# Flamingo layer with routed zones: a ring of eight places for the zone weights, four fixed loads a body, and the last body's weights scaled while they are rounded

## The chip, the cores and the metric

The kernel runs on one core of a Trainium2 chip. What counts is the device time of one execution in microseconds (us), as the median of several runs. Engines are named as in the profile: PE is TensorE (PEld its weight loads), DVE VectorE, ACT ScalarE, POOL GpSimd, SP SyncE, which here only issues DMAs; "SPq" rows are those issues.

## What is computed

For 8 images: a layer norm, cross attention of 112 queries to 375 context rows (16 heads of 16), a gated residual; then a layer norm, a router that picks 3 of 8 zones per image, and for each of them a hidden layer of 1024 with Gelu, weighted and added.

```python
x = x + tanh(g_xattn[0]) * xattn(layernorm(x), ctx, ctx, mask, Wq, bq, Wk, bk, Wv, bv, Wo, bo)
# _L0_ffn_ref(x): called with layernorm(x)
pooled = x.mean(axis=1)
h = jnp.tanh(pooled @ W1 + b1)
logits = h @ W2 + b2
probs = jax.nn.softmax(logits, axis=-1)
top_p, top_i = jax.lax.top_k(probs, TOP_K)
top_w = top_p / top_p.sum(axis=-1, keepdims=True)
for e in range(N_ZONES):
    z = jax.nn.gelu(x @ Wa[e]) @ Wb[e]
    zone_outputs = zone_outputs + z * w[:, e, None, None]
x = x + tanh(g_ffn[0]) * (x + zone_outputs)
```

x is 8 x 112 x 256, Wa is 8 x 256 x 1024 and Wb 8 x 1024 x 256, all in float32. The products need more than float16's precision, so keys, queries, the hidden layer and the zone weights are held as two float16 numbers, a high part (the value rounded) and a low part (what the rounding left).

## The kernel before, in words

**Two phases.** In the first, attention runs image by image while all zone weights are fetched, scaled by 64 (WSCALE) and split into high and low halves in SBUF (`wa`, `wb`). In the second, 24 pairs of image and zone run one after the other: `g1` (L1370) and `g2` (L1397) are 48 matmuls each of 128x128 by 128x112.

**Bodies and slots.** The first phase is a loop over b from -1 to 7, written out by hand for every engine; each engine has its own instruction stream and waits on semaphores. A body has four slots. In slot s of body b TensorE makes the transposed scores of image b for one group of heads (`st_tile`, L1159 and L1163, three tiles), the plain scores of image b+1 (`s1`, L1147), from which VectorE takes row maxima (L866), the product with the values (`pv`, L1181), and some small work of images b+2, b and b-1 between (context transposes L1190, key and query projections L1199 and L1225, value projection L1208 and others). ScalarE does the exponentials (L597).

**Keys and queries through DRAM.** The keys of image b+2 are projected in slots 0 and 1 of body b. ScalarE rounds them (L697), VectorE makes the low part (`k_lo`, L908), SP writes both to DRAM (`write_k`, L341, one call for each half) and reads them back in another layout (`read_k`, L352, and `read_q`, L305). The first `s1` of body b+1 needs the reads of heads 0 to 7 of image b+2. The row maxima take a like way: ScalarE copies them to `ms`, SP copies them into `rq` (`move_max`, L361), and `st_tile` of the next body reads `rq` in L1159.

**Zone weights.** The weights are 64 parts of 128 x 512 float32, eight per zone: four of Wa, four of Wb. A load (`load_parts`, L373 for Wa, L376 for Wb) brings two parts, 512 KB, into two places of the ring `stage`, which has six. For each part GpSimd scales it in place (`scale_part`, L503, one slot ahead), ScalarE rounds it into `wa` or `wb` (`w_hi`, L707), and GpSimd subtracts the rounded from the scaled (`lo_part`, L508), which frees the place. Each slot of bodies 0 to 7 finishes two parts; parts 56 to 63 (LATE and on) belong to body 7, and their low parts are made by VectorE (`lo_late`, L961). SP calls `load_parts` four times a body, two slots ahead of ScalarE; each call waits until the two places are free. SP works its stream strictly in order, so what stands behind a waiting call waits as well.

**The seam.** After body 7 everything waits for the last weights. VectorE reads the number of the first zone from `idx_row` into a register (L996, in `copy_weights`), copies that zone's Wa from `wa` to `wqkvo` and `qbd` (L998 and L999), and TensorE starts `g1(0)`. `hidden` on ScalarE does the Gelu (L800) and the weighting (L802).

## Time and profile before

| what | value |
|---|---|
| median of 3 runs | 319.05 us (318.33 to 320.27) |
| the profiled execution | 319.47 us |
| its span in the profile | 317.7 us |
| TensorE matmul busy | 293.0 us (92%) |
| VectorE, ScalarE busy | 227.3 us, 223.8 us |
| GpSimd busy | 136.4 us |
| moved by DMA | 40.59 MB |

The profile comes from one execution. Times in its rows are microseconds from the start of the span, durations in the rows of single instructions too, those called mean or given as min/median/max are nanoseconds. "[2.02 <-DMA qbd<-q_scr]" at a row's end means that the engine stood idle for 2.02 us before it, and that the transfer from `q_scr` to `qbd` ended this. The rows of a timeline merge instructions that follow each other directly (x24). PEclk is TensorE's granted clock, 1.00 (or a digit of 9) for 2.4 GHz and 0.50 for 1.2 GHz; over a stretch it is a mean. "issue" is idle time in which the engine waited for nothing that the profile shows.

Bodies begin, counted by TensorE's first L1147 in them, at 53.74 (body 1), 75.16 (2), 96.77 (3), 117.53 (4), 138.36 (5) and 159.04 us (6); the last body has no L1147 and begins at 175.7.

### The profile page before, as it was taken

To read this page: it belongs to the slowest core of one execution; us is meant where nothing else is said; L and a number is where in the kernel's file an instruction comes from. 1 tells how busy PE (TensorE), PEld (TensorE's weight loads), DVE (VectorE), ACT (ScalarE), POOL (GpSimd) and SP (SyncE) were. 2 spreads that over 40 slices of the span, in tenths; PEclk is the share of its full clock that TensorE was granted. 3 is DMA by queue.
4 is the path that set the end of the run, shared out by engine and by line. 5 is a ranking of instruction groups with operands and counts; after the bars stand their busy time and mean duration, and the time that the engine had idled before them with its cause. 6 is when DMAs were issued, how large, how long until landed. Compare 5 with 4: busy or idle time off the path is not lost.

```text
span 317.7 us, 10417 instructions
## 1 busy us (share of the span) xinstructions
PE 293.0 (92%) x3968; PEld 242.0 (76%) x3968; DVE 227.3 (72%) x648; ACT 223.8 (70%) x439; POOL 136.4 (43%) x191
## 2 busy tenths in 40 slices
PE   7876997997999999999899876999999999999996
PEld 6642675775777767777567556999999999999996
DVE  5359685675787986879667675886886878767773
ACT  3541775884888878788677874867676976766773
POOL 4493385867769867688489541000100000000000
PEclk9995799998999999999999997999999999999999
DMA  6468978875878897777964550110211001010101
GB/s 167 122 181 222 261 181 230 218 208 150 219 188 237 209 268 203 197 192 204 226 161 135 174 155 2 32 31 2 62 32 32 23 25 47 2 46 5 31 2 31
DMA packets 38417, 40.59 MB, mean 128 GB/s; under 512 B 9800, under 2 KB 34032, under 8 KB 38368
## 3 DMA queue, kind: packets, MB, share of 16 engines
q1 hardware_dynamic: 37216, 38.48, 44.7%
q0 software_dynamic: 608, 0.92, 1.1%
q8 instruction: 32, 0.52, 0.7%
q10 hardware_dynamic: 544, 0.52, 0.5%
q14 instruction: 17, 0.14, 0.1%
HBM read 33.09 MB, written 6.74 MB: 125 GB/s over the span
## 4 chain that ended last, share of the span: by engine, by line
PE 61%; DMA 17%; DVE 7%; SPq 5%; ACT 4%; issue 4%; POOL 1%; DVEq 0%; ACTq 0%
PE bank L1370 17%; PE bank L1397 16%; DMA k_scr<-wb 8%; PE bank L1199 5%; DMA qbd<-q_scr 4%; PE bank L1181 4%; PE bank L1147 4%; PE bank L1159 3%; PE bank L1163 3%; SPq L352 2%; PE bank L1190 2%; DMA stage<-in_L_ffn_Wa 2%; DVE bank L866 2%; DMA ctx_s<-in_ctx 1%; PE bank L1208 1%
## 5 line engine op out<-in xcount | busy, mean ns | idle before, releaser
L866 DVE CUSTOM_DVE_ANT_0 bank<-bank,maskb 112x375 f32<-112x375 f32 x128 | 67.8, 569 | 27.1 <-PE bank L1147 26.6
L1370 PE MATMUL bank<-ctxT,wqkvo 128*128 128x112 f16 x960 | 60.9, 215 | 5.3 <-DVE qbd L999 5.3
L1370 PEld LDWEIGHTS bank<-ctxT,wqkvo 128*128 128x128 f16 x960 | 57.8, 99 | 6.0 <-issue 6.0
L1397 PE MATMUL bank<-stage,pT 128*128 128x112 f16 x1104 | 58.1, 213 | 0.0
L597 ACT ACTIVATE pT<-bank 125x448 f32<-125x448 f32 x96 | 50.2, 538 | 9.8 <-PE bank L1163 9.4
L1397 PEld LDWEIGHTS bank<-stage,pT 128*128 128x128 f16 x1104 | 55.8, 98 | 0.3
L503 POOL TENSOR_SCALAR stage<-stage 128x512 f32<-128x512 f32 x64 | 39.2, 629 | 37.0 <-DMA stage<-in_L_ffn_Wa 25.4
L1147 PE MATMUL bank<-kst,qbd 128*112 128x375 f16 x128 | 36.0, 350 | 10.2 <-DMA qbd<-q_scr 6.0
L1370 PE MATMUL bank<-ctxT,qbd 128*128 128x112 f16 x192 | 41.3, 215 | 0.0
L1159 PE MATMUL bank<-rq,maskb 115*128 115x448 bf16 (+1 forms) x96 | 35.9, 374 | 1.8 <-ACT pT L597 1.1
L812 ACT ACTIVATE pT<-wb 128x1024 f16 x23 | 24.3, 1056 | 15.9 <-PE bank L1397 13.8
L998 DVE COPY wqkvo<-wa 128x3072 f16 x24 | 23.0, 960 | 16.8 <-PE bank L1370 14.9
L1163 PE MATMUL bank<-qbd,kst 128*128 128x224 f16 (+1 forms) x192 | 34.9, 263 | 0.0
L508 POOL TENSOR_TENSOR wa<-stage,wa 128x512 f16<-128x512 f32 x28 | 32.0, 1163 | 4.3 <-ACT wa L707 4.3
L802 ACT ACTIVATE stage<-kst,wbc 128x448 f16<-128x448 f32 x48 | 32.1, 669 | 1.6
L1082 DVE SCALAR_TENSOR_TENSOR stage<-kst,wbc,stage 128x448 f16<-128x448 f32 x48 | 32.6, 678 | 0.6 <-ACT stage L802 0.6
L508 POOL TENSOR_TENSOR wb<-stage,wb 128x512 f16<-128x512 f32 x28 | 31.8, 1156 | 0.2 <-ACT wb L707 0.2
L1010 DVE COPY pT<-wb 128x3072 f16 x23 | 22.1, 959 | 12.6 <-PE bank L1397 12.6
L1163 PEld LDWEIGHTS bank<-qbd,kst 128*128 128x128 f16 (+1 forms) x192 | 21.8, 113 | 12.0 <-issue 1.9
L1147 PEld LDWEIGHTS bank<-kst,qbd 128*112 128x112 f16 x128 | 15.0, 133 | 18.4 <-DVE peaks L866 9.5
L800 ACT ACTIVATE kst<-bank 128x448 f32<-128x448 f32 x48 | 25.5, 531 | 2.5 <-PE bank L1370 2.5
L513 POOL TENSOR_TENSOR rstd<-ve,half 112x1 f32<-112x1 f32 x16 | 8.8, 550 | 38.5 <-DVE ve L888 38.5
(143 smaller groups left out, 495.0 us busy)
## 6 DMA issues: line engine op xcount, KB each, us to landing
stage<-in_L_ffn_Wa SPq DMA_DIRECT2D x16, 512.0 KB, 4.8
stage<-in_L_ffn_Wb SPq DMA_DIRECT2D x16, 512.0 KB, 4.1
kst<-k_scr SPq DMA_DIRECT2D x64, 93.8 KB, 3.8
k_scr<-wb SPq DMA_DIRECT2D x16, 187.5 KB
ctx_s<-in_ctx SPq DMA_DIRECT2D x8, 336.0 KB
qbd<-q_scr SPq DMA_DIRECT2D x24, 56.0 KB, 3.3
xa<-in_x SPq DMA_DIRECT2D x8, 112.0 KB, 4.7
q_scr<-wb SPq DMA_DIRECT2D x16, 56.0 KB, 3.4
```

The lines of the kernel that those rows point to most:

```text
L503: g.tensor_scalar(st, st, WSCALE, 1.0, ALU.mult, ALU.mult).then_inc(s["scaled"], 1)
L508: g.tensor_tensor(part_dst(k, 1), stage[:, k % RING, :], part_dst(k, 0), ALU.subtract).then_inc(s["lo_done"], 1)
L597: a.activation(pT[0:CK, t % PRING, :], bank[0:CK, ST_BANKS[t % len(ST_BANKS)], 0:QUAD], ACT.Exp).then_inc(s["act_exp"], 1)
L800: a.activation(h_w[:, cols], bank[:, 2 * (u % 2) + hf, 0:QUAD], ACT.Gelu_apprx_tanh, scale=1.0 / WSCALE).then_inc(s["gelu_done"], 1)
L802: a.activation(hT[:, u % 2, cols], h_w[:, cols], ACT.Copy, scale=wbc[:, u:u + 1]).then_inc(s["hthi_done"], 1)
L866: v.tensor_tensor_reduce(out=bank[0:SQ, e, 0:SK], in0=bank[0:SQ, e, 0:SK], in1=maskb[0:SQ, b % 2, 0:SK], scale=-1.0, scalar=FLOOR, op0=ALU ...
L1082: v.scalar_tensor_tensor(out=hT[:, u % 2, (2 + hf) * QUAD:(3 + hf) * QUAD], in0=h_w[:, cols], scalar=wbc[:, u:u + 1], in1=hT[:, u % 2, col ...
L1147: T.matmul(bank[0:SQ, e, 0:SK], qbd[:, b % 2, e, p, :], kst[:, b % 2, p * SK:(p + 1) * SK], start=True, stop=True).then_inc(s["pe_s1"], 1)
L1159: T.matmul(o[0:w, :].rearrange("k (j q) -> k j q", j=4), maskb[0:KQ, b % 2, c * CK:c * CK + w], rq[0:KQ, g // 2, :, g % 2, :], start=True, ...
L1163: ins = T.matmul(o[0:w, i * 2 * SQ:(i + 1) * 2 * SQ].rearrange("k (e q) -> k e q", e=2), kst[:, b % 2, p * SK + c * CK:p * SK + c * CK + w ...
L1370: ins = T.matmul(o, first(ws, t, f), x2b[:, b % 2, (xs * DT + t) * SQ:(xs * DT + t + 1) * SQ], start=(t == 0 and xs == 0 and ws == 0), sto ...
L1397: ins = T.matmul(o, second(u, ws * (2 * CHUNK) + f * D + t * 128), hT[:, u % 2, hs * FT * SQ + f * SQ:hs * FT * SQ + (f + 1) * SQ], start= ...
```

## The change

The ring gets eight places (RING), of which six are in `stage` (STAGES). Places 6 and 7 are guests: in the low half of zone 7's Wa, which is written only in body 7, and for the last pair of parts (62 and 63) in the half of `kst` that held the keys of image 6; that load waits until image 6's scores are done. `in_ring` gives the address of a place.

SP's loads stand at fixed places of a body now, each under the number of its pair of parts. Two follow each other at a body's head (pairs 4b+2 and 4b+3), one stands behind the query write and in front of `move_max`, one behind `read_q`. Before, the second stood in front of the key writes and the third behind `move_max`.

Parts 56 to 63 are no longer scaled by GpSimd: ScalarE waits for the load and rounds with a scale of 64, and VectorE computes 64 x raw minus rounded in one instruction. VectorE reads the first zone's number between its low parts of slots 2 and 3 of the last body. ScalarE gets a Gelu of a spent 112 x 1 column before the wait for the last weights, and with it the table load.

```diff
@@ -35,7 +35,7 @@
 PARTS = 8
 NPART = NZ * PARTS
 LATE = NPART - 8
-RING = 6
+RING, STAGES = 8, 6
 PRING = 5
 ROUTES = ((0, B - 3), (B - 3, 3))
 VC = HD + 1
@@ -166,7 +166,7 @@
         wa = sb("wa", [128, NZ * 2 * DT * FF], F16)
         wb = sb("wb", [128, NZ * 2 * FT * D], F16)
-        stage = sb("stage", [128, RING, PART])
+        stage = sb("stage", [128, STAGES, PART])
         wqkvo = sb("wqkvo", [128, 4, DT, D])
         bq_c = sb("bq_c", [128, DT])
         bk_c = sb("bk_c", [128, DT])
@@ -291,6 +291,15 @@
             at = z * (4 * CHUNK) + hl * (2 * CHUNK) + (q % 4) * PART
             return t[:, at:at + PART]
+        def in_ring(k, n=1):
+
+            i = k % RING
+            if i < STAGES:
+                return stage[:, i:i + n, :].rearrange("p a f -> p (a f)")
+            i -= STAGES
+            home = wa[:, (NZ - 1) * 4 * CHUNK + 2 * CHUNK:] if k < LATE else kst[:, 0, :]
+            return home[:, 2 * PART * i:2 * PART * (i + n)].bitcast(F32)
+
         def full(eng, name):
             eng.wait_ge(s["misc_full"], spare.full(name))
@@ -361,20 +370,21 @@
                     sp.dma_start(rq[SQ:KQ, h, :, :, :].rearrange("c j g q -> c (j g q)"),
                                  ms[:, h, :, :].rearrange("r g q -> r (g q)")).then_inc(rq_in[h], 16)
-            def load_parts(b, slot):
-
-                for k in parts_at(b + (slot + 2) // 4, (slot + 2) % 4)[::2]:
+            def load_pair(p):
+
+                k = 2 * p
+                if k < NPART:
                     z, q = k // PARTS, k % PARTS
-                    i = k % RING
                     need(sp, s["lo_done"], min(k - RING + 2, LATE))
                     need(sp, s["lo_late"], k - RING + 2 - LATE)
-                    dst = stage[:, i:i + 2, :]
+                    if k >= LATE and k % RING >= STAGES:
+                        sp.wait_ge(s["pe_st"], tile(B - 1, 0, 0))
+                    dst = in_ring(k, 2)
                     if q < 4:
-                        sp.dma_start(dst.rearrange("p a f -> p (a f)"),
-                                     Wa[z, (q // 2) * 128:(q // 2) * 128 + 128, :]).then_inc(part_loaded[i // 2], 16)
+                        sp.dma_start(dst, Wa[z, (q // 2) * 128:(q // 2) * 128 + 128, :]).then_inc(part_loaded[k % RING // 2], 16)
                     else:
-                        sp.dma_start(dst.rearrange("p a (f n) -> p (a f) n", n=D),
-                                     Wb[z, (q - 4) * 256:(q - 2) * 256, :].rearrange("(f p) n -> p f n", p=128)).then_inc(part_loaded[i // 2], 16)
+                        sp.dma_start(dst.rearrange("p (f n) -> p f n", n=D),
+                                     Wb[z, (q - 4) * 256:(q - 2) * 256, :].rearrange("(f p) n -> p f n", p=128)).then_inc(part_loaded[k % RING // 2], 16)
             def load_xr(b):
                 if there(b):
@@ -442,18 +452,22 @@
                     read_k(n, 1)
                     read_q(sp, n, 1)
                 move_max(b, 1)
-                load_parts(b, 0)
+                if b >= 0:
+                    load_pair(4 * b + 2)
+                    load_pair(4 * b + 3)
                 load_xr(o)
                 if b >= 0:
                     load_ctx(m + 1)
                     load_x(m + 1)
                 load_mask(m)
-                load_parts(b, 1)
                 write_k(m, 0)
                 write_k(m, 1)
                 write_q(m)
+                if b >= 0:
+                    load_pair(4 * b + 4)
                 move_max(n, 0)
-                load_parts(b, 2)
+                if b == -1:
+                    load_pair(0)
                 if b == B - 1:
                     store_index(0)
                     sp.wait_ge(s["xt_done"], B)
@@ -466,7 +480,7 @@
                     read_k(1, 1)
                 read_k(m, 0)
                 read_q(sp, m, 0)
-                load_parts(b, 3)
+                load_pair(4 * b + 5)
                 store_r(b - 2)
                 store_x2(b - 2)
             load_xr(B - 1)
@@ -498,14 +512,14 @@
             def scale_part(k):
-                st = stage[:, k % RING, :]
+                st = in_ring(k)
                 pool.wait_ge(part_loaded[k % RING // 2], 16 * (k // RING) + 16)
                 g.tensor_scalar(st, st, WSCALE, 1.0, ALU.mult, ALU.mult).then_inc(s["scaled"], 1)
             def lo_part(k):
                 pool.wait_ge(s["hi_done"], k + 1)
-                g.tensor_tensor(part_dst(k, 1), stage[:, k % RING, :], part_dst(k, 0), ALU.subtract).then_inc(s["lo_done"], 1)
+                g.tensor_tensor(part_dst(k, 1), in_ring(k), part_dst(k, 0), ALU.subtract).then_inc(s["lo_done"], 1)
             def norm(ve_, nm_, rstd_, nmr_, ready, n, signal):
@@ -566,7 +580,8 @@
                     if (b, slot) == (-1, 3):
                         norm1(2)
                     for k in parts_at(b + (slot + 1) // 4, (slot + 1) % 4):
-                        scale_part(k)
+                        if k < LATE:
+                            scale_part(k)
                     if slot == 0:
                         norm2(b - 2)
                     if slot == 2:
@@ -703,8 +718,11 @@
                         act.wait_ge(k_written[0], 16 * B)
                         act.wait_ge(k_written[1], 16 * B)
                         act.wait_ge(s["q_written"], 32 * B)
-                    act.wait_ge(s["scaled"], k + 1)
-                    a.activation(part_dst(k, 0), stage[:, k % RING, :], ACT.Copy).then_inc(s["hi_done"], 1)
+                    if k < LATE:
+                        act.wait_ge(s["scaled"], k + 1)
+                    else:
+                        act.wait_ge(part_loaded[k % RING // 2], 16 * (k // RING) + 16)
+                    a.activation(part_dst(k, 0), in_ring(k), ACT.Copy, scale=1.0 if k < LATE else WSCALE).then_inc(s["hi_done"], 1)
             def route_hidden(g):
@@ -825,6 +843,7 @@
                     a.activation(o_sb[:, at + lo * SQ:at + hi * SQ].rearrange("p (t f) -> p t f", f=SQ), bank[:, 4 + lo:4 + hi, 0:SQ], ACT.Copy).then_inc(s["yt_done"], 1)
             o_copy(B - 1)
+            a.activation(nm[:, :], nm[:, :], ACT.Gelu_apprx_tanh)
             act.wait_ge(s["lo_done"], LATE)
             act.wait_ge(s["lo_late"], NPART - LATE)
             hidden(0)
@@ -957,8 +976,11 @@
                 if b == B - 1:
                     for k in parts_at(b, slot):
+                        if k == LATE:
+                            dve.wait_ge(s["lo_done"], LATE)
                         dve.wait_ge(s["hi_done"], k + 1)
-                        v.tensor_tensor(part_dst(k, 1), stage[:, k % RING, :], part_dst(k, 0), ALU.subtract).then_inc(s["lo_late"], 1)
+                        v.scalar_tensor_tensor(out=part_dst(k, 1), in0=in_ring(k), scalar=WSCALE, in1=part_dst(k, 0),
+                                               op0=ALU.mult, op1=ALU.subtract).then_inc(s["lo_late"], 1)
             def route_logits(g):
@@ -989,15 +1011,16 @@
                 full(dve, ("W", g))
                 v.tensor_copy(wbc[:, b0 * TOPK:(b0 + n) * TOPK], spare_bank(("W", g))[:, 0:n * TOPK]).then_inc(s["wbc_done"], 1)
-            def copy_weights(u):
-
+            def zone(u):
                 if u == ROUTES[1][0] * TOPK:
                     dve.wait_ge(s["idx_loaded"], 32)
-                e = dve.value_load(idx_row[0:1, u:u + 1], min_val=0, max_val=NZ - 1)
+                return dve.value_load(idx_row[0:1, u:u + 1], min_val=0, max_val=NZ - 1)
+
+            def copy_weights(u, e):
+
                 need(dve, s["g1_done"], 2 * u)
                 v.tensor_copy(wst3, wa[:, bass.ds(e * (4 * CHUNK), 3 * CHUNK)]).then_inc(s["wst_done"], 1)
                 v.tensor_copy(wst1, wa[:, bass.ds(e * (4 * CHUNK) + 3 * CHUNK, CHUNK)]).then_inc(s["wst_done"], 1)
-                return e
             def stay(u, e):
@@ -1054,15 +1077,17 @@
                 row_max(n, 6)
                 row_max(n, 7)
                 split_max(n, 1)
+                if b == B - 1:
+                    dve.wait_ge(s["idx_loaded"], 16)
+                    e = zone(0)
                 lo_late(b, 3)
                 if b == B - 1:
-                    dve.wait_ge(s["idx_loaded"], 16)
                     dve.wait_ge(s["hi_done"], NPART)
                     dve.wait_ge(s["lo_done"], LATE)
                     dve.wait_ge(s["lo_late"], NPART - LATE)
                     full(dve, ("V1", B - 1))
                     dve.wait_ge(s["pe_st"], tile(B - 1, 0, 0))
-                    e = copy_weights(0)
+                    copy_weights(0, e)
                 residual(o)
                 if b == 0:
                     dve.wait_ge(s["const_loaded"], 80)
@@ -1094,7 +1119,9 @@
             for u in range(B * TOPK):
                 b, k = u // TOPK, u % TOPK
-                nxt = copy_weights(u + 1) if u + 1 < B * TOPK else None
+                nxt = zone(u + 1) if u + 1 < B * TOPK else None
+                if nxt is not None:
+                    copy_weights(u + 1, nxt)
                 low(u, 0)
                 stay(u, e)
                 low(u, 1)
```

**Order of SP's issues in a body.** SP's stream from the head of body 5 in the kernel before: `rq<-ms` is `move_max`, `stage<-` the weight loads, `k_scr<-wb` and `q_scr<-wb` the key and query writes, `kst<-k_scr` and `qbd<-q_scr` the reads.

```order
L361 DMA rq<-ms 3x4x224
L376 DMA stage<-in_L_ffn_Wb 128x4x256
L382 DMA xr<-in_x 112x256
L329 DMA mask_s<-in_mask_Bx1xSxS_bk 112x375
L376 DMA stage<-in_L_ffn_Wb 128x4x256
L341 DMA k_scr<-wb 8x32x375 x2
L335 DMA q_scr<-wb 128x2x112 x2
L361 DMA rq<-ms 3x4x224
L373 DMA stage<-in_L_ffn_Wa 128x1024
L352 DMA kst<-k_scr 32x1500 x4
L305 DMA qbd<-q_scr 64x1x448 x2
L373 DMA stage<-in_L_ffn_Wa 128x1024
```

The same piece in the changed kernel, where `wa<-in_L_ffn_Wb` is a load into the guest places:

```order
L370 DMA rq<-ms 3x4x224
L386 DMA stage<-in_L_ffn_Wb 128x4x256
L386 DMA wa<-in_L_ffn_Wb 128x4x256
L392 DMA xr<-in_x 112x256
L338 DMA mask_s<-in_mask_Bx1xSxS_bk 112x375
L350 DMA k_scr<-wb 8x32x375 x2
L344 DMA q_scr<-wb 128x2x112 x2
L384 DMA stage<-in_L_ffn_Wa 128x1024
L370 DMA rq<-ms 3x4x224
L361 DMA kst<-k_scr 32x1500 x4
L314 DMA qbd<-q_scr 64x1x448 x2
L384 DMA stage<-in_L_ffn_Wa 128x1024
```

The second Wb load has moved up behind the first; the Wa load stands in front of `rq<-ms` and no longer behind it.

**GpSimd at the end of body 6 and in body 7.** The kernel before, from the low parts of slot 2 of body 6 on; L503 is the scaling, L508 the low part, L513 and L514 a norm, L528 adds the output bias:

```order
L508 TENSOR_TENSOR wb<-stage,wb 128x512 x2
L503 TENSOR_SCALAR stage<-stage 128x512 x2
L508 TENSOR_TENSOR wb<-stage,wb 128x512 x2
L503 TENSOR_SCALAR stage<-stage 128x512 x2
L513 TENSOR_TENSOR rstd<-ve,half 112x1
L514 TENSOR_TENSOR nmr<-nm,rstd 112x1
L503 TENSOR_SCALAR stage<-stage 128x512 x4
L528 TENSOR_TENSOR xr<-xr,bo_r 112x256
```

The changed kernel, from the same instruction on:

```order
L522 TENSOR_TENSOR wb<-stage,wb 128x512 x2
L522 TENSOR_TENSOR wb<-wa,wb 128x512 x2
L527 TENSOR_TENSOR rstd<-ve,half 112x1
L528 TENSOR_TENSOR nmr<-nm,rstd 112x1
L542 TENSOR_TENSOR xr<-xr,bo_r 112x256
```

The scalings of 56 to 63 (x2, x2 and x4) are gone; the low parts of 54 and 55 and the norm follow directly.

**VectorE at the seam.** The kernel before, from the low part of the transposed x2 (L952) in body 7 to the copy for the first zone (L998); L996 reads the zone's number, L961 are low parts:

```order
L952 TENSOR_TENSOR x2T<-bank,x2T 128x224
L953 TENSOR_REDUCE pooled<-bank 128x2
L961 TENSOR_TENSOR wb<-stage,wb 128x512 x4
L996 TENSOR_LOAD idx_row
L996 ISA x2
L998 ISA
L998 COPY wqkvo<-wa 128x3072
```

And the changed kernel, L982 being the low parts:

```order
L971 TENSOR_TENSOR x2T<-bank,x2T 128x224
L972 TENSOR_REDUCE pooled<-bank 128x2
L982 SCALAR_TENSOR_TENSOR wb<-stage,wb 128x512 x2
L1017 TENSOR_LOAD idx_row
L1017 ISA x2
L982 SCALAR_TENSOR_TENSOR wb<-kst,wb 128x512 x2
L1022 ISA
L1022 COPY wqkvo<-wa 128x3072
```

Reading the number has moved in front of the last two low parts; behind them the copy follows.

## Rows read from the trace of the kernel before

**Rows 1.** The page: busy time by engine, and the granted clock in 40 slices.

```profile
PE 293.0 (92%) x3968; PEld 242.0 (76%) x3968; DVE 227.3 (72%) x648; ACT 223.8 (70%) x439; POOL 136.4 (43%) x191
...
PEclk9995799998999999999999997999999999999999
```

**Rows 2.** Waits of TensorE: us in total, times, longest us.

```profile
PE bank L1147 <- DMA qbd<-q_scr: 6.0, 4, 2.0
```

**Rows 3.** TensorE in order of time: start, us, engine, line, operation.

```profile
53.74 0.53 PE L1147 MATMUL bank<-kst,qbd 128*112 128x375 f16 x2 [1.75 <-DMA qbd<-q_scr]
...
75.16 0.53 PE L1147 MATMUL bank<-kst,qbd 128*112 128x375 f16 x2 [2.02 <-DMA qbd<-q_scr]
...
157.00 0.35 PE L1159 MATMUL bank<-rq,maskb 115*128 115x448 bf16 x1
...
159.04 0.53 PE L1147 MATMUL bank<-kst,qbd 128*112 128x375 f16 x2 [1.49 <-DMA qbd<-q_scr]
```

**Rows 4.** Windows: PE PEld DVE ACT POOL busy (x instructions), PEclk, DMA share, GB/s.

```profile
76.00:80.00 4.00, 4.00 (x41) 3.50 (x41) 1.56 (x7) 2.40 (x6) 1.90 (x4) 0.57 0.25 46
141.00:143.00 2.00, 2.00 (x12) 1.29 (x11) 0.64 (x4) 1.71 (x5) 1.38 (x3) 1.00 0.24 46
153.00:160.00 7.00, 5.51 (x59) 3.81 (x60) 4.63 (x18) 4.21 (x11) 2.94 (x5) 1.00 1.03 265
192.00:196.00 4.00, 3.57 (x42) 3.60 (x43) 1.64 (x7) 1.07 (x1) 1.42 (x3) 0.57 0.01 4
```

**Rows 5.** TensorE in order of time, around the seam.

```profile
188.38 0.77 PE L1181 MATMUL bank<-pT,vp 125*17 125x112 f32 x24
...
192.43 0.62 PE L1370 MATMUL bank<-ctxT,wqkvo 128*128 128x112 f16 x5 [3.29 <-DVE qbd L999]
```

**Rows 6.** The chain that ended last: start, us, what.

```profile
29.77 2.02 DMA rq<-ms
...
43.19 6.04 DMA k_scr<-wb
...
147.80 4.46 DMA k_scr<-wb
```

**Rows 7.** The DMA issues of SP in order of time.

```profile
41.53 0.40 SPq L376 DMA_DIRECT2D stage<-in_L_ffn_Wb  x1
...
144.23 0.39 SPq L376 DMA_DIRECT2D stage<-in_L_ffn_Wb  x1
...
148.44 1.01 SPq L335 DMA_DIRECT2D q_scr<-wb  x2
...
150.71 0.42 SPq L373 DMA_DIRECT2D stage<-in_L_ffn_Wa  x1
...
153.16 1.23 SPq L305 DMA_DIRECT2D qbd<-q_scr  x2
```

**Rows 8.** Waits of SP's DMA queue: us in total, times, longest us.

```profile
SPq L376 <- POOL wa L508: 11.2, 7, 3.4
```

**Rows 9.** The tile stage: its DMAs from issue to landing.

```profile
DMA to landing us min/median/max: 3.9/4.4/6.6
```

**Rows 10.** VectorE in order of time, around the seam.

```profile
186.38 3.30 DVE L961 TENSOR_TENSOR wb<-stage,wb 128x512 f16<-128x512 f32 x4
...
190.99 0.96 DVE L998 COPY wqkvo<-wa 128x3072 f16 x1 [1.31 <-issue]
...
196.65 0.96 DVE L998 COPY wqkvo<-wa 128x3072 f16 x1 [2.87 <-PE bank L1370]
```

**Rows 11.** The page, part 5: count, busy us, mean ns, idle before.

```profile
L1082 DVE SCALAR_TENSOR_TENSOR stage<-kst,wbc,stage 128x448 f16<-128x448 f32 x48 | 32.6, 678 | 0.6 <-ACT stage L802 0.6
```

**Rows 12.** ScalarE in order of time, around the seam.

```profile
186.70 1.19 ACT L707 ACTIVATE wb<-stage 128x512 f16<-128x512 f32 x2
...
187.74 0.58 ACT L597 ACTIVATE pT<-bank 125x448 f32<-125x448 f32 x1
...
194.93 1.28 ACT L800 ACT_TABLE_LOAD   x1 [5.17 <-PE bank L1370]
```

More of the change, by code:

```diff
@@ L258, in flamingo_layer @@
                  "k_written0 k_written1 q_written kq_in00 kq_in01 kq_in10 kq_in11 q_first00 q_first01 q_first10 q_first11 r_written x2_written "
-                 "part_loaded0 part_loaded1 part_loaded2 scaled hi_done lo_done lo_late "
+                 "part_loaded0 part_loaded1 part_loaded2 part_loaded3 scaled hi_done lo_done lo_late "
                  "pe_s1 pe_st pe_pv misc_full dve_max act_exp act_o parts_done ms_done rq_in0 rq_in1 xr_ready "
```

## The prediction

> **What bounds the kernel now.** I read the page first: TensorE is busy for 293.0 us of a span of 317.7 [rows 1], so only what makes it stand still, or run at its lower clock, can be won back. Next the waits by engine and TensorE's rows in order of time. Inside the attention bodies one kind stands out: the first score matmul of a body (L1147) waits for keys and queries read back from DRAM, 6.0 us in four places [rows 2]. Three are shown: 1.75, 2.02 and 1.49 us [rows 3]; the fourth is the rest, 0.74. The reader should then look at the granted clock behind each. After the 2.02 us it fell: from 76 to 80 us TensorE was busy all the time at 0.57 of the full clock [rows 4], so (1 - 0.57) x 4.0 = 1.7 us of work were lost; behind the shorter gaps of 1.75 and 1.49 us (slices 7 and 21 of 40) the page's row of clocks stays at 9 [rows 1]. The same price stands at 192 to 196 us [rows 4], behind the longest gap of all: TensorE ends the attention at 188.38 + 0.77 = 189.15 and begins the zones at 192.43, 3.29 us [rows 5]. From there on it is nearly always busy. So the change can win in two places: the body starts (6.0 + 1.7 us) and the seam before the zones (3.3 + 1.7 us).
>
> **The loads within a body.** The chain shows what the body start at 159.04 waits for: key half 1 is written to DRAM at 147.80 and takes 4.46 us, until 152.26 [rows 6]; only then its reads are issued, and the queries' two at 153.16 to 154.39 [rows 7], which land at 159.0, 4.6 us after the last issue. The DMA share says why that is slow: from 141 to 143 us the 16 engines were 0.24 busy, from 153 to 160 full, 1.03 [rows 4]. In the idle stretch SP stood at the second Wb load until GpSimd had emptied a ring place, at 144.23 [rows 7]; it did so 7 times, 11.2 us in all [rows 8]. In the full stretch the Wa load of 150.71 moves beside the keys.
>
> With eight places the second Wb load goes out right behind the first, about 142 instead of 144.23. The key and query writes keep their times, since VectorE's low halves release them. Only in body 0 the wait for the place lasted to 41.53 [rows 7], and the key write behind it took 6.04 instead of 4.46 us [rows 6]: 1.5 us should go. The Wa load now goes out when the query write's issue ends, 148.44 + 1.01 = 149.45, instead of 150.71 [rows 7]: 1.26 us sooner, and as the engines are full from 153 on, what is in front of the keys is less by what moved in that time. The four waits by this: 1.75 - 1.5 = 0.25; 2.02 - 1.1 (the same distance in that body) = 0.9; 0.74 to 0; 1.49 - 1.26 = 0.2. That is 4.6 us less, and behind a gap of 0.9 us the clock should hold, 1.7 more: 6.3. I take three quarters, 4.7, since the other engines' work is nearly as long as a body and some of their waits will come due. Bounds: nothing won, if what has to move before the keys is the same; at most all, 7.7.
>
> A body still moves the same bytes. Inputs and context of later images now stand behind 1 MB of weights instead of 0.5, about 2 us later (half of the median landing of 4.4 us, [rows 9]); they are used half a body or a body later, so that is nothing; without this cover it would be up to 2 us where VectorE's layer norm waits. Two ring places lie as guests in the low half of zone 7's Wa, and for the last pair in old keys: all SBUF, so nothing either way. VectorE's new wait before the low half of part 56 is for GpSimd's part 55, which comes sooner than before, as 56 and 57 are no longer scaled ahead of it; key sums that could queue behind it don't exist in the last body. Nothing.
>
> **The last body.** GpSimd's eight scalings go; ScalarE multiplies while it rounds (the same instruction with another scale: nothing), and VectorE's low halves become a multiply-subtract. The trace has none of 512 columns: the four subtractions took 3.30 us together [rows 10], the nearest multiply-subtract, of 448 columns, 678 ns [rows 11]; by columns 775 ns, against 3.30/4 = 825 for what it replaces, stretched by GpSimd's work beside it. So between -0.05 and +0.1 each; I take +0.05, of which the last two lie on the path: +0.1. ScalarE is what this body ends on: two roundings from 186.70, then the last exponential from 187.74 [rows 12], on which the last product (188.38) waits. It never waited long for GpSimd; I take 0.25 us for a norm that stood behind the scalings (0 to 0.5).
>
> **The seam.** Before: VectorE's low halves ran from 186.38 to 189.68; then 1.31 us without work (waits, and reading the zone's number for an address), the copy at 190.99, and TensorE 1.44 us behind the copy's start [rows 5, 10]. After: both Wb pairs are in the ring about 185, the last two parts are rounded from 186.70 to 187.89 [rows 12] as before. VectorE does parts 60 and 61 from 186.4 to 187.8, reads the zone's number behind them in the queue while it works, and 62 and 63 until 189.0; 0.15 us for the waits left; 1.44 us: TensorE at 190.6, minus 0.25, plus 0.1: 190.45. That is 1.98 us sooner, the last body's gain included. The gap left is 190.45 - 188.9 = 1.55 us, less than the 1.75 behind which the clock held, so the slow start's 1.7 goes too: 3.7 us. If reading the number isn't hidden, 0.9 comes back, the gap is 2.4, the clock falls as it did after 2.02, and 1.1 are left. So the seam brings 1.1 to 4.0.
>
> The early Gelu moves a table load of 1.28 us [rows 12] out of the first zone. I cost it at nothing: TensorE's next wait (until 198.09) ended with VectorE's copies for the second zone, begun at 196.65 after 2.87 us of waiting for TensorE itself [rows 10].
>
> **Sum.** 4.7 + 3.7 = 8.4 us off the profiled execution, 319.47 us for its span of 317.7: 311.1. The median of the runs lies 0.4 below the profiled one: 310.7.
>
> **A rule against the change.** The small copy of the row maxima took 2.02 us to land with little in front of it [rows 6]; now it is issued behind a weight load of 512 KB, at about 149.9. The Trainium skill (DMA: Bandwidth & Descriptors, Queues, rings and completion order) says that an issuing engine has one ring on each of the 16 DMA engines, and that each consumes its descriptors in ring order. By that rule the maxima land with the load and not 2 us after their issue; no row here has them in this order. What that would do is the third rival.
>
> **Rivals.** First: only the seam is won. For it: the DMA engines are full from 153 to 160 us, and a body with shorter waits presses them more. Against: they were idle at 141 to 143. Bodies 1.0 (two thirds of body 0's write), seam 2.7 (the middle, the clock in doubt): 319.05 - 3.7 = 315.3. Second: the change frees nothing that counts; body waits come back at other engines and the seam keeps a gap of over 2 us: 1.1 in all, 317.9. For it: the last body ends on ScalarE, which does as much as before. Against: SP's 11.2 us of waits are real, and the keys stand behind them. Third, slower: the maxima. The first tile of each of seven bodies needs them; this one ran at 157.00 [rows 3]. With the load landing after 4.4 us they are there at 153.9, after 6.6 (the longest, [rows 9]) at 156.1. It decides from a landing of 157.00 - 149.45 = 7.55 us on. At 9.5 TensorE would wait 2 us at seven starts, 14 us, which take today's 6.0 with them: +8, less the seam's 3.7: 323.4.
>
> **Chances.** Forecast with its spread 0.65, first rival 0.22, second 0.08, third 0.05. About 1% (3.2 us) is what a measurement of this kernel can tell from no change. The first rival straddles that line (315.9), two thirds of it on the faster side. Faster 0.65 + 0.15 = 0.80; within 1% 0.07 + 0.08 = 0.15; slower 0.05. The range runs from 319.05 - 7.7 - 4.0 = 307.4 to bodies of 1.5 and a seam of 1.1, 316.5.
>
> **What would show it.** Right: L1147's waits for the queries sum to about 1.4 us; no stretch at the lower clock behind the second of them; SP without waits for GpSimd at the weight loads; TensorE's gap before the zones at 1.3 to 1.7 us with the full clock behind it; VectorE's copy some 0.2 us behind its last low half. Wrong: waits of L1159 for the maxima; key waits unchanged though the load leaves sooner; a gap of over 2 us at the seam; a new wait of ScalarE for the last Wb pair.

## The result, and the profile after

The changed kernel takes 310.15 us in the median (309.97 to 311.1, 4 runs), the kernel before in the same session 318.69; the ratio is 0.9732 with a 95% interval of 0.9689 to 0.9775. That is 2.7% faster; the forecast was 310.7. The profiled execution takes 310.05 us (span 308.1) against 319.47 (317.7), so the traces have 9.6 us of span to explain. Here and below medians are over all runs, while the ratios, each to the kernel before in the same session, leave out single runs that fell into a slower state.

I cut both traces at four places that TensorE's rows give: the first tile of the last body (L1159, after the change L1186; the first one behind the router's first matmul), the end of the last `pv`, the first matmul of zone 0 and that of zone 1. What lies behind zone 1's start did not change, the four stretches in front of it did:

| stretch, us | before | after |
|---|---|---|
| to the first tile of the last body | 175.67 | 169.86 |
| last body | 13.48 | 13.12 |
| gap before the zones | 3.28 | 1.46 |
| first zone until the second starts | 5.66 | 4.12 |
| the rest | 119.61 | 119.54 |

So 5.8 us came from all that stands in front of the last body and 3.7 from the last body and the seam (0.36, 1.82 and 1.54). The page of the changed kernel, parts 1 and 2, against [rows 1]:

```profile
PE 289.6 (94%) x3968; PEld 240.5 (78%) x3968; DVE 227.9 (74%) x648; ACT 223.2 (72%) x440; POOL 131.0 (43%) x183
...
PEclk9997699999999999999999999999999999999999
```

The engines' work is the same but for GpSimd's eight scalings. In the row of clocks the 8 of slice 10 and the 7 of slice 25 are gone; what the row still shows at the lower clock lies in the start. TensorE's waits in the changed kernel (us, times, longest), against [rows 2]:

```profile
PE bank L1174 <- DVE peaks L885: 4.4, 8, 1.5
...
PE bank L1186 <- DMA rq<-ms: 1.0, 1, 1.0
...
PE bank L1174 <- DMA qbd<-q_scr: 0.6, 2, 0.3
```

L1174 is the first score matmul, L1147 before. Its wait for the queries fell from 6.0 us to 0.6. The 1.0 us for `rq` lies in the start, at 32.37, where the kernel before waited 0.5 us for the same; of the 4.4 us for VectorE's maxima 3.2 lie in the start, as before, and 1.1 are new in the bodies (0.88 us at 86.12, 0.26 at 146.03). The two waits that are left, in TensorE's timeline, against [rows 3]:

```profile
53.02 0.53 PE L1174 MATMUL bank<-kst,qbd 128*112 128x375 f16 x2 [0.30 <-DMA qbd<-q_scr]
...
72.63 0.53 PE L1174 MATMUL bank<-kst,qbd 128*112 128x375 f16 x2 [0.27 <-DMA qbd<-q_scr]
```

SP's issues in body 5 of the changed kernel, against [rows 7]: the second Wb load (into `wa`, a guest place) stands directly behind the first, the Wa load directly behind the query write.

```profile
138.11 0.50 SPq L386 DMA_DIRECT2D wa<-in_L_ffn_Wb  x1
...
144.22 1.01 SPq L344 DMA_DIRECT2D q_scr<-wb  x2
145.28 0.47 SPq L384 DMA_DIRECT2D stage<-in_L_ffn_Wa  x1
145.84 0.79 SPq L370 DMA_DIRECT2D rq<-ms  x1
```

And SP's waits for GpSimd, 2.5 us in place of the 15.6 of three such rows before (one of them [rows 8]):

```profile
SPq L386 <- POOL wa L522: 1.3, 1, 1.3
SPq L384 <- POOL wa L522: 1.2, 1, 1.2
```

The seam, first TensorE's timeline, then VectorE's, then ScalarE's, against [rows 5, 10, 12]:

```profile
182.21 0.77 PE L1208 MATMUL bank<-pT,vp 125*17 125x112 f32 x24
184.44 0.41 PE L1397 MATMUL bank<-ctxT,wqkvo 128*128 128x112 f16 x5 [1.46 <-DVE qbd L1023]
```

```profile
180.21 1.29 DVE L982 SCALAR_TENSOR_TENSOR wb<-stage,wb 128x512 f16<-128x512 f32 x2
181.41 1.29 DVE L982 SCALAR_TENSOR_TENSOR wb<-kst,wb 128x512 f16<-128x512 f32 x2
183.00 0.96 DVE L1022 COPY wqkvo<-wa 128x3072 f16 x1 [0.30 <-issue]
```

```profile
180.54 1.19 ACT L725 ACTIVATE wb<-kst 128x512 f16<-128x512 f32 x2
181.58 0.58 ACT L612 ACTIVATE pT<-bank 125x448 f32<-125x448 f32 x1
...
183.61 1.28 ACT L846 ACT_TABLE_LOAD   x1
```

VectorE starts its copy 0.30 us behind the last low part instead of 1.31, and the four low parts take 2.49 us instead of 3.30. TensorE's five first matmuls of the zone take 0.41 us; before they took 0.62, at the lower clock.

### The profile page after: what moved, and what is told of

The parts are those of the page before. It is cut to its first block and busy times, and to the rows that moved or that the text cites. A ratio compares the mean times of both kernels' runs of the same rounds, so it can differ in the third digit from the quotient of the medians.

```text
span 308.1 us, 10410 instructions
## 1 busy us (share of the span) xinstructions
PE 289.6 (94%) x3968; PEld 240.5 (78%) x3968; DVE 227.9 (74%) x648; ACT 223.2 (72%) x440; POOL 131.0 (43%) x183
## 3 DMA queue, kind: packets, MB, share of 16 engines
HBM read 33.09 MB, written 6.74 MB: 129 GB/s over the span
## 5 line engine op out<-in xcount | busy, mean ns | idle before, releaser
L1397 PE MATMUL bank<-ctxT,wqkvo 128*128 128x112 f16 x960 | 59.4, 213 | 3.5 <-DVE qbd L1023 3.5
L1397 PEld LDWEIGHTS bank<-ctxT,wqkvo 128*128 128x128 f16 x960 | 56.5, 98 | 4.2 <-issue 4.2
L1174 PE MATMUL bank<-kst,qbd 128*112 128x375 f16 x128 | 35.6, 344 | 6.5 <-DVE peaks L885 4.4
L517 POOL TENSOR_SCALAR stage<-stage 128x512 f32<-128x512 f32 x42 | 25.4, 623 | 28.8 <-DMA stage<-in_L_ffn_Wa 23.8
L1186 PE MATMUL bank<-rq,maskb 115*128 115x448 bf16 (+1 forms) x96 | 35.9, 374 | 1.7 <-DMA rq<-ms 1.0
L1174 PEld LDWEIGHTS bank<-kst,qbd 128*112 128x112 f16 x128 | 15.0, 131 | 14.4 <-DVE peaks L885 11.8
L1208 PE MATMUL bank<-pT,vp 125*17 125x112 f32 (+1 forms) x768 | 24.7, 261 | 0.1
```

The source lines that it names most:

```text
L517: g.tensor_scalar(st, st, WSCALE, 1.0, ALU.mult, ALU.mult).then_inc(s["scaled"], 1)
L1174: T.matmul(bank[0:SQ, e, 0:SK], qbd[:, b % 2, e, p, :], kst[:, b % 2, p * SK:(p + 1) * SK], start=True, stop=True).then_inc(s["pe_s1"], 1)
L1186: T.matmul(o[0:w, :].rearrange("k (j q) -> k j q", j=4), maskb[0:KQ, b % 2, c * CK:c * CK + w], rq[0:KQ, g // 2, :, g % 2, :], start=True, ...
L1397: ins = T.matmul(o, first(ws, t, f), x2b[:, b % 2, (xs * DT + t) * SQ:(xs * DT + t + 1) * SQ], start=(t == 0 and xs == 0 and ws == 0), sto ...
```

## The experiments

Eleven kernels. Their times scatter more than the effect of the smaller edits, so I cut every trace as above. The diffs show the lines that matter, shortened, against the changed kernel; the remarks behind # are added. One reading has to be kept in mind: the first phase is the same in the changed kernel, e7, e8, e10 and e11 up to the last body, or nearly so, and its end came at 169.86, 170.37, 168.49, 170.33 and 171.49 us. That is a spread of 3.0 us, so one pair of traces can't tell a difference below about 3 us in this stretch. Part of the spread is the clock of the start. Its mean from 15 to 45 us is 0.83 in five traces (before, changed, e1, e5, e8) and 0.77 in the other eight; the changed kernel, then e11:

```profile
15.00:45.00 30.00, 23.51 (x141) 13.65 (x144) 20.58 (x77) 14.81 (x35) 17.69 (x30) 0.83 0.83 218
15.00:45.00 30.00, 24.49 (x124) 13.78 (x122) 20.30 (x76) 14.34 (x34) 18.00 (x31) 0.77 0.81 219
```

By these means the lower clock lasted about 10 us in the one group and 14 in the other, which is up to 1.8 us of work (0.06 x 30). The seam stretches repeat to 0.1 us. The kernel before took 318.98 us in the session of e1 to e4, 317.6 in that of e5 to e8 and 318.81 in that of e9 to e11; the changed kernel itself was run in an earlier session (before: 318.69), so times are best compared within a session or by their ratios.

| kernel | median, us | ratio to before | first tile of last body | last body | gap | zone 0 to 1 |
|---|---|---|---|---|---|---|
| changed | 310.15 | 0.973 (0.969 to 0.978) | 169.86 | 13.12 | 1.46 | 4.12 |
| e1 | 313.3 | 0.983 (0.974 to 0.992) | 169.24 | 14.01 | 2.31 | 5.49 |
| e2 | 314.79 | 0.989 (0.984 to 0.994) | 175.68 | 13.55 | 1.30 | 4.12 |
| e3 | 315.06 | 0.989 (0.984 to 0.993) | 172.89 | 13.24 | 2.73 | 4.11 |
| e4 | 323.15 | 1.018 (1.010 to 1.027) | 177.86 | 13.89 | 3.07 | 5.41 |
| e5 | 312.58 | 0.986 (0.981 to 0.991) | 173.55 | 13.11 | 1.46 | 4.11 |
| e6 | 310.84 | 0.981 (0.977 to 0.984) | 169.66 | 13.12 | 1.46 | 4.11 |
| e7 | 312.76 | 0.984 (0.979 to 0.989) | 170.37 | 13.11 | 2.47 | 4.12 |
| e8 | 311.38 | 0.984 (0.978 to 0.989) | 168.49 | 13.12 | 1.52 | 4.12 |
| e9 | 322.86 | 1.016 (1.008 to 1.023) | 182.87 | 13.12 | 1.46 | 4.12 |
| e10 | 311.11 | 0.981 (0.975 to 0.987) | 170.33 | 13.99 | 1.30 | 4.11 |
| e11 | 310.58 | 0.977 (0.970 to 0.984) | 171.49 | 13.11 | 1.13 | 4.12 |

**e1, the ring and its order alone.** The changed kernel with the last body as before:

```diff
+                        scale_part(k)                      # parts 56 to 63 too
+                    act.wait_ge(s["scaled"], k + 1)
+                        v.tensor_tensor(part_dst(k, 1), in_ring(k), part_dst(k, 0), ALU.subtract)
+                    e = zone(0)                            # behind the last low parts
-            a.activation(nm[:, :], nm[:, :], ACT.Gelu_apprx_tanh)
```

> The change's ring of eight and its order of loads alone; the last body's scaling on GpSimd, the zone's number read late and the Gelu late, as before. Theory of the prediction: the bodies win all they won with the whole change (5.8 us in the traces of before and after), the waits of the first score matmul for the queries fall from 6.0 to about 0.6 us, and at the seam the last Wb pair is early but still scaled by GpSimd: gap about 2.4 us, slow clock behind it, 1 us won there. 318.7 - 6.8 = 311.9 us. Rival 1, the bodies' gain comes with the last body's parts too: 315 us. Rival 2, the seam's gain is the ring's as well (the load was what came late): gap 1.5 us, clock full, 310.2 us.

Measured 313.3 us. The last body begins at 169.24, within the scatter of the changed kernel's 169.86: the bodies' gain is the ring's and its order's, and rival 1 falls. The gap is 2.31 us with the lower clock behind it, so rival 2 falls as well. TensorE's timeline and a window of e1:

```profile
185.56 0.41 PE L1390 MATMUL bank<-ctxT,wqkvo 128*128 128x112 f16 x5 [2.30 <-DVE qbd L1017]
```

```profile
186.00:190.00 4.00, 4.00 (x47) 3.88 (x43) 1.18 (x6) 2.63 (x4) 1.42 (x3) 0.57 0.01 4
```

**e2, the last body alone.** The changed kernel with six places and the loads where they stood:

```diff
-RING, STAGES = 8, 6
+RING, STAGES = 6, 6
-                    load_pair(4 * b + 3)                   # at the head
+                    load_pair(4 * b + 3)                   # in front of write_k
-                    load_pair(4 * b + 4)                   # in front of move_max
+                load_pair(4 * b + 4)                       # behind move_max
```

> The change's last body alone: scaling while rounding, the number early, the Gelu early; ring of six places and the loads where they stood before. Theory: bodies as before (6.0 us of waits for queries), at the seam the last Wb pair is issued once two late low parts are done, about 3 us after the body's head, but isn't scaled by GpSimd any more: it is rounded in time, gap about 1.5 us, full clock: 3.8 us won, 314.9 us. Rival: the load comes too late for ScalarE, which waits for it; gap over 2 us, clock falls, 1.5 us won, 317.2 us.

Measured 314.79 us against 314.9 expected; the first phase ends at 175.68, where it ended before (175.67), the gap is 1.30 us. That the two ends agree so well is luck: e2 began body 0 2.0 us later (first score matmul at 34.59 against 32.57) and spent 2.0 us less from there. The seam's gain doesn't need the ring: the late load is in time once GpSimd doesn't have to scale it. e1 and e2 add up within their intervals: 1.7% and 1.1% against 2.7% for the whole.

The last body takes 13.55 us here, 0.4 more than in the changed kernel, for a reason of its own. A step of the router on VectorE came while GpSimd added the output bias (183.10 to 183.83), and took 0.70 us; in the changed kernel the same step took 0.22:

```profile
183.15 0.70 DVE L997 TENSOR_SCALAR pz<-ez,few 5x8 f32<-5x8 f32 x1
```

**e3, eight places in the old order.** As e1, with the two loads moved as in e2.

> Eight places, but each load at its old place in SP's order (second Wb load in front of the key writes, first Wa load behind the maxima); last body as before. Theory of the prediction (two causes: SP no longer stands for a place, and the Wa load goes out 1.3 us sooner): only body 0's write gains, 1.5 us, and the query waits stay near 4 us: 318.7 - 1.5 - 1.0 (seam) = 316.2 us. Rival (what counts is that SP doesn't stand; the order is worth nothing): as e1, 311.9 us.

Measured 315.06 us, last body from 172.89. By the traces eight places win 2.8 of e1's 6.4 us by themselves and the order 3.6. But e3 has the longer low clock in the start and e1 the shorter, so up to 1.8 us of the 3.6 may be that; the split is a rough one. The waits for queries, 3.5 us in e3 against 0.2 in e1, show that the order counts; those of the old order on six places, 6.0 us before and 4.4 in e2, show the part of the places less clearly:

```profile
PE bank L1165 <- DMA qbd<-q_scr: 3.5, 3, 1.6
```

**e4, the new order on six places.** As e1 with `RING, STAGES = 6, 6`.

> The new order of loads on six places; last body as before. SP now stands for a place at the body's head, in front of inputs, mask and key writes. Theory: GpSimd frees that place about 3 us after the head of a body; keys are written about when they were before, inputs later; the Wa load gains its 1.3 us but SP's stand at the head costs body 0 as before: 316 to 318 us. Rival, order is all: 312 us. Other rival, slower: the inputs and masks behind the stand make a body longer, 320 us or more.

Measured 323.15 us, slower than before: the slower rival. SP now stands at the body's head with inputs, mask and key writes behind it. Its waits in e4:

```profile
SPq L386 <- POOL wa L522: 23.0, 7, 5.4
SPq L384 <- POOL wb L522: 4.0, 2, 2.9
SPq L384 <- POOL wa L522: 2.9, 2, 2.7
```

That is 29.9 us of waiting in place of 15.6. The order costs time without the places; the places without the order (e3) give a part of the gain.

**e5, the Wa load behind the maxima again.** Which of the two moves is worth 3.6 us?

```diff
-                    load_pair(4 * b + 4)
                 move_max(n, 0)
+                load_pair(4 * b + 4)
```

> The changed kernel (310.15 us) with the first Wa load behind the copy of the maxima again, the second Wb load still at the body's head. With eight places and the old order (e3) the last body began at 172.9 us of the span, with the new order (e1) at 169.2: one of two moves is worth 3.6 us. Theory A, it is this one (the Wa load's 512 KB leave 1.3 us later and stand in front of the keys at four body starts): waits for queries rise to 3 to 4 us, last body from 172.5 to 173 us, time 313.5 us. Theory B, it is the second Wb load's: this kernel stays at 310.2 to 311 us, waits for queries below 1.5 us.

Measured 312.58 us, last body from 173.55 against 169.86: theory A. The trace shows more than the runs do: e5's profiled execution (313.74 us) lies 1.2 us above its median. Against e6, which has the Wa load in front of the maxima and ran in the same session, e5 is 1.7 us slower in the median and 2.3 in the mean. Body 0 shows the effect alone, since up to there the two streams are level to 0.25 us. SP in the changed kernel, then in e5, then TensorE's wait in e5:

```profile
46.54 0.47 SPq L384 DMA_DIRECT2D stage<-in_L_ffn_Wa  x1
47.10 0.77 SPq L370 DMA_DIRECT2D rq<-ms  x1
...
49.83 1.25 SPq L314 DMA_DIRECT2D qbd<-q_scr  x2
```

```profile
46.74 0.78 SPq L370 DMA_DIRECT2D rq<-ms  x1
47.56 0.41 SPq L384 DMA_DIRECT2D stage<-in_L_ffn_Wa  x1
...
49.95 1.25 SPq L314 DMA_DIRECT2D qbd<-q_scr  x2
```

```profile
54.81 0.53 PE L1171 MATMUL bank<-kst,qbd 128*112 128x375 f16 x2 [1.99 <-DMA qbd<-q_scr]
```

The load leaves 1.02 us later, the query reads are issued 0.12 us later and take 4.0 us to land instead of 2.6 (medians of the two), and TensorE begins at 54.81 instead of 53.02. The DMA engines between show it (DMA share and GB/s last), first the changed kernel, then e5:

```profile
46.00:49.00 3.00, 1.00 0.74 175
49.00:53.00 4.00, 1.00 0.76 208
```

```profile
46.00:49.00 3.00, 1.00 0.58 115
49.00:53.00 4.00, 1.00 0.89 237
```

In e5 the engines are emptier while there is nothing else to do and fuller while keys and queries come. Why 1.0 us of lead is worth 1.8 us of landing these rows don't explain.

**e6, the second Wb load in front of the key writes again.** The other move of e2's diff.

> The changed kernel with the second Wb load at its old place, behind inputs and mask and right in front of the key writes; the Wa load in front of the maxima. It waits for nothing now and leaves 2 to 3 us later than in the changed kernel only by what stands in front of it (1.7 to 2.5 us). Theory A: nothing lost, last body from about 170 us, 310.2 us. Theory B (the load's 512 KB stand in front of the key writes on the same DMA engines): key writes take longer by up to 1.5 us, waits for queries 3 us or more, 313.5 us.

Measured 310.84 us, last body from 169.66, waits for queries in e6:

```profile
PE bank L1175 <- DMA qbd<-q_scr: 0.8, 2, 0.5
```

Theory A: with eight places this load may stand at either place.

**e7, the zone's number late.**

```diff
                 lo_late(b, 3)
+                    e = zone(0)
```

> The changed kernel with the zone's number read behind the last low parts, as before. Theory of the prediction: 0.9 to 1.0 us come back between VectorE's last low part and its copy, the gap before the zones is 2.4 us. After such a gap the clock fell in e1 (2.31 us) and held in e3 (2.73 us); if it falls 1.4 to 1.7 us more: 311.2 us with the clock held, 312.7 us with it fallen. Rival: the number's read is hidden anyway, 310.2 us.

The gap is 2.47 us, 1.01 more than in the changed kernel: the first step as expected. In this trace the clock held. TensorE's timeline and a window of e7:

```profile
185.95 0.41 PE L1396 MATMUL bank<-ctxT,wqkvo 128*128 128x112 f16 x5 [2.47 <-DVE qbd L1023]
```

```profile
186.00:190.00 4.00, 2.91 (x52) 2.67 (x52) 2.54 (x9) 2.47 (x5) 1.42 (x3) 1.00 0.02 4
```

It held behind 2.73 us in e3 too, and fell behind 2.31 us in e1. The median, 312.76 us with runs from 310.76 to 315.92, doesn't decide which happens more often.

**e8, the Gelu late.** The changed kernel without the added activation.

> The changed kernel without the early Gelu, so that the table load stands in the first zone again. Theory of the prediction: nothing, the second zone's first matmul waits for VectorE's copy, and the second products find their low parts in time: 310.2 us, first zone to second 4.12 us as with it. Rival: VectorE's copy for the second zone waits behind what ScalarE releases, 1.2 us: 311.4 us.

ScalarE's timeline of e8 has the table load in the first zone:

```profile
184.62 1.28 ACT L818 ACT_TABLE_LOAD   x1 [2.40 <-PE bank L1396]
```

The second zone begins 4.12 us behind the first, as with the early Gelu: nothing won or lost. The median, 311.38 us, is 1.2 above the changed kernel's, as the rival has it, but from another session. e6, which has the early Gelu, took 310.84 us in the same session, with a ratio of 0.981 against 0.984, and e8's own profiled execution took 308.75, less than any run of the changed kernel. So the runs don't tell the two apart, and the trace shows no place for 1.2 us.

**e9, both Wa loads in front of the maxima.**

```diff
                     load_pair(4 * b + 4)
+                    load_pair(4 * b + 5)
                 move_max(n, 0)
...
-                load_pair(4 * b + 5)                       # behind read_q, from body 0 on
```

> The changed kernel with the second Wa load (behind the query reads until now) put in front of the maxima as well, so that 1 MB and not 512 KB stand in front of the maxima, keys and queries. Theory A (the bytes in front of the reads decide; 512 KB are 2 us at the 265 GB/s of the full stretch): queries land about 2 us later, waits of 1.5 to 2 us at five or six starts, 8 to 10 us in all, minus some clock: 319 to 321 us, and the maxima may be what the first tile waits for. Theory B (what hurt was a load in flight beside the reads, and a load well ahead of them doesn't): waits below 2 us, 310 to 311.5 us.

Measured 322.86 us, last body from 182.87, 13 us later than in the changed kernel. TensorE's waits in e9:

```profile
PE bank L1176 <- DMA qbd<-q_scr: 9.6, 6, 2.5
...
PE bank L1188 <- DMA rq<-ms: 3.1, 4, 1.4
```

Theory A: the bytes in front of the reads decide. In body 0 the two query reads take 5.1 us to land (median), 2.6 in the changed kernel. Here the first tile waits for the maxima as well. Of the 3.1 us, 1.4 are the wait in the start that the changed kernel has too (1.0); the other three, 1.7 us, are new. The first of them, SP's issue and then TensorE's tile:

```profile
48.22 0.78 SPq L370 DMA_DIRECT2D rq<-ms  x1
```

```profile
53.81 0.35 PE L1188 MATMUL bank<-rq,maskb 115*128 115x448 bf16 x1 [0.81 <-DMA rq<-ms]
```

SP also stood 4.7 us for a ring place once, in body 6; the last body, which follows it, begins without a wait.

**e10, GpSimd scales the last parts again.** The first three lines of e1's diff.

> The changed kernel, but GpSimd scales the last body's eight parts again and VectorE subtracts; ring, order, early number and early Gelu stay. Theory of the prediction: 0.25 us of a norm behind the scalings, otherwise hidden since the pairs come early: gap 1.5 us, 310.4 us. Rival from e1 (where the last body was 14.01 us and not 13.12): 0.9 us come back in the last body, since ScalarE and VectorE wait for GpSimd: 311.1 us.

Measured 311.11 us; the last body takes 13.99 us and not 13.12, the gap 1.30 and not 1.46, so 0.7 us come back in all. The place is not the one expected. TensorE waits for the router's weights (`wdiag`, L1001), and VectorE's small steps to them are stretched; VectorE in e10 with the page's wait of TensorE for it, then the same two steps in the changed kernel:

```profile
178.93 0.57 DVE L999 TENSOR_SCALAR wz<-ptop,few 5x3 f32<-5x3 f32 x1
179.54 0.55 DVE L1001 TENSOR_TENSOR wdiag<-wz,ident 5x15 f32<-5x15 f32 x1
```

```profile
PE bank L1318 <- DVE wdiag L1001: 1.0, 1, 1.0
```

```profile
178.28 0.22 DVE L1004 TENSOR_SCALAR wz<-ptop,few 5x3 f32<-5x3 f32 x1
178.53 0.16 DVE L1006 TENSOR_TENSOR wdiag<-wz,ident 5x15 f32<-5x15 f32 x1
```

In e10 GpSimd scales beside them, from 177.31 to 180.07 but for 0.1 us. In e3 GpSimd scales as well, but both steps fell into a pause between its pairs and took 0.22 and 0.16 us; its last body is 13.24 us. Last body and gap together, GpSimd's scalings cost 0.7 us in e10 (15.29 against 14.58 in the changed kernel) and 0.4 in e3 (15.97 against 15.58 in e7, which reads the number late too).

**e11, the first matmuls before the small copy.** An attempt to go further:

```diff
-                pe.wait_ge(s["wst_done"], 2 * u + 2)
+                pe.wait_ge(s["wst_done"], 2 * u + 1)
+                            if f == 0 and t == 1 and ws == 1:
+                                pe.wait_ge(s["wst_done"], 2 * u + 2)
```

> The changed kernel with one thing more: TensorE begins a zone's first product when VectorE's big copy is done and waits for the small one only before the first matmul that reads it. Theory: at the seam and before the second zone five matmuls move into the small copy's 0.42 us, 0.25 us each, nothing later: 309.6 to 310 us, gap before the zones 1.2 us instead of 1.46. Rival: the first product can't start earlier since the wait costs as much at its new place: 310.2 us.

TensorE's timeline of e11:

```profile
185.73 0.41 PE L1399 MATMUL bank<-ctxT,wqkvo 128*128 128x112 f16 x5 [1.13 <-DVE wqkvo L1022]
```

The gap is 1.13 us instead of 1.46 and the stretch behind zone 1's start is 118.95 us instead of 119.54, so the trace shows 0.9 us. The runs (median 310.58 us, 307.98 to 312.83) scatter too much to confirm it: this kernel isn't shown to beat the changed one.

## Why the prediction was right, and where its steps were not

**The two places.** The forecast of 310.7 us rested on 4.7 us from the bodies and 3.7 from last body and seam. Measured in the traces: 5.8 and 3.7. e1 and e2 show them apart and adding up.

**The waits in the bodies.** Forecast: 1.4 us of waits for queries left, of 6.0; measured 0.6. The 1.7 us of lower clock behind the second start came back. I had taken three quarters of the sum for what would come due at other engines; TensorE's waits for VectorE's row maxima in the bodies grew from nothing to 1.1 us, so the discount was the right kind and somewhat too large. A start that came 0.5 us later than before (first score matmul of body 0 at 33.09 against 32.57) took a little more.

**Body 0.** The step that failed is "the key write behind it took 6.04 instead of 4.46 us: 1.5 us should go", once the second Wb load no longer waits for its place. In e5 that load is out of the way just as well, and the wait behind body 0 is 1.99 us, no less than the 1.75 before. The write did get shorter: in e5 it had landed within 4.9 us of its issue at 44.04, since its reads go out without a pause. But the two query reads behind it took 4.0 us to land in place of 2.8 (medians), and the gain was gone. What removes the wait is the Wa load's lead, the step that I gave 1.1 to 1.26 us each at the other starts and nothing at this one. By e5 a lead of 1.02 us let the queries of body 0 land 1.79 us sooner; until the last body it was worth 3.7 us in the traces and about 2 in the runs. That the sum for the bodies still came close is in part luck: body 0's remaining wait came out as forecast, 0.30 us for 0.25, with the gain put down to the wrong load.

**The stand of SP.** That the 11.2 us stood in front of what matters was half right. Eight places with the old order give 2.8 us in the trace (e3), less than the scatter of that stretch. Once SP doesn't stand, where the second Wb load is doesn't matter (e6).

**The rivals.** First (only the seam): fell, the DMA engines had room before the full stretch. Second: fell. Third (the maxima behind a load): it didn't decide in the changed kernel, where no tile waits for them behind the start. With twice the bytes in front they come too late (e9): issued at 48.22 behind two loads, they released the tile at 53.81, 5.6 us later and not 2.02 as in [rows 6]. That is the direction of the rule on ring order that I set against the change; its price in e9 is 1.7 us at three body starts.

**The last body.** The cost of the multiply-subtract, +0.05 us each, was nothing: two take 1.29 us, like two subtractions (1.29 us in e10). The gain of dropping GpSimd's scalings, 0.25 us "for a norm", had the wrong reason: e10 shows 0.87 us in this body, by VectorE's small router steps, and e3 0.12, where these steps ran undisturbed. Between before and after it is 0.36, since in the kernel before VectorE's last two router steps ran in GpSimd's pause between its last two pairs of scalings.

**The seam.** Forecast gap 1.55 us, measured 1.46; reading the number early was forecast at 0.9 us and measured at 1.01 (e7); the early Gelu at nothing, and nothing was seen (e8).

**The clock.** The result was right and the reason weak: a gap "less than the 1.75 behind which the clock held". It held behind 2.47 (e7) and 2.73 us (e3), and fell behind 2.31 (e1) and 2.02. So the length of one gap doesn't decide it here. All thirteen traces together say more. Behind the eight seams with a gap of 1.13 to 1.52 us the clock held every time, and the first zone took 4.11 or 4.12 us; behind the five with 2.31 to 3.28 us it fell three times (before, e1, e4) and held twice (e3, e7). The changed kernel's 1.5 us of gain at zone 0 is measured, and that a shorter gap makes it likelier is supported by this count; how often the clock would have held anyway stays open.

## What to carry to other kernels

A load that must move anyway belongs where the queue's engines would be idle just before the reads that the next stage waits for: 1 us earlier was worth about 2 us in the runs and 3.7 in the traces here, and 512 KB more in front cost 13. Such a place is only good with buffers enough that the issuing engine hardly stands there; the same order on six places was 1.8% slower than before. Cut each trace at fixed instructions when runs scatter: stretches of 13 and 4 us repeated to 0.1 us where whole runs of one kernel differed by 5. The longer stretch in front of them scattered by 3 us, and a difference read from it needs the runs of the same session beside it.

## What the runs showed of the hardware that was not expected

VectorE's steps on 5 x 3 and 5 x 15 numbers took 0.57 and 0.55 us beside GpSimd's scaling and 0.22 and 0.16 without it (e10 and the changed kernel). Each ended within 0.02 us of the end of a GpSimd instruction that ran beside it. The Trainium skill (SBUF — State Buffer, SBUF: two separate sides) states that VectorE and GpSimd share a port pair which one of them holds for a whole instruction, for VectorE when it runs a two-port mode or has two operands in SBUF. The second step has two such operands and agrees. The first has one, and a second that is a single number per row; whether that one counts, or the step ran in a two-port mode, no run here tells.

The granted clock fell or held behind gaps of 1.9 to 2.7 us with no order by their length: it fell behind 1.94 (e4), 2.02 (before), 2.19 (e2), 2.31 (e1) and 2.55 us (e9), and held behind 1.99 (e5), 2.14 (e9), 2.47 (e7) and 2.73 us (e3).
